# One copy and a DMA for the rows of negative maxima, a lead of seven heads, and the bins' fills on SyncE

## The reference

```python
x = x + L0_xattn(layernorm(x), ctx, mask_BxSxS2_bf1)      # 2 heads of 64
x = x + L0_ffn(layernorm(x))                              # token mix, sigmoid gate, relu squared
x = x + L1_xattn(layernorm(x), ctx, ctx, mask_Bx1xSxS2)   # 16 heads of 8
x = x + L1_ffn(layernorm(x))                              # 8 experts, each token goes to one
```

```python
scores = jnp.einsum('bhsd,bhtd->bhst', qh, kh) / math.sqrt(8)
scores = jnp.where(mask == 0, -1e9, scores)
attn = jax.nn.softmax(scores, axis=-1)                    # over 512 keys
out = jnp.einsum('bhst,bhtd->bhsd', attn, vh)
```

## Time and profile before

| | us |
|---|---|
| median of 3 runs | 298.65 |
| the three runs | 297.97, 298.65, 302.39 |
| span of the profiled execution (first to last instruction) | 296.5 |
| TensorE busy | 258.6 (87%) |
| VectorE busy | 187.7 (63%) |
| ScalarE busy | 144.1 (49%) |
| GpSimd busy | 92.3 (31%) |
| L700, the copy of the rows, 16 of them | 16.0 |
| L716, exp, 64 of them | 65.2 |

### The profile page before, as it was taken

How to read it: one execution, slowest core, us unless ns; L and a number is a source line. 1 busy time by engine, 2 the same in 40 slices (tenths; PEclk the granted TensorE clock), 3 DMA queues, 4 the chain that set the end, 5 groups by cost and what they waited for, 6 DMA issues and landing times.

```text
span 296.5 us, 5874 instructions
## 1 busy us (share of the span) xinstructions
PE 258.6 (87%) x2048; PEld 129.6 (44%) x2048; DVE 187.7 (63%) x659; ACT 144.1 (49%) x273; POOL 92.3 (31%) x108
## 2 busy tenths in 40 slices
PE   0799998697598999999998999999999888959991
PEld 0345666365353344444433334332444345625550
DVE  3290966849889767678778568664777146724440
ACT  1178465524045656656466356562576533414440
POOL 2643692603403400003300112000214642577533
PEclk9999999879799999999999799995999999988997
DMA  6990456241464689620004999520101893369500
GB/s 177 410 413 20 123 133 158 53 133 35 108 160 110 149 263 271 147 88 2 0 2 143 308 419 309 135 70 9 38 0 37 302 367 85 100 182 362 181 20 7
DMA packets 20812, 44.69 MB, mean 151 GB/s; under 512 B 1670, under 2 KB 15757, under 8 KB 19824
## 3 DMA queue, kind: packets, MB, share of 16 engines
q1 hardware_dynamic: 9296, 30.63, 32.5%
q10 hardware_dynamic: 9824, 10.00, 12.8%
q0 software_dynamic: 1664, 3.69, 3.5%
HBM read 30.90 MB, written 13.93 MB: 151 GB/s over the span
## 4 chain that ended last, share of the span: by engine, by line
PE 47%; DVE 8%; ACT 7%; issue 4%; DMA 3%; POOL 1%; POOLq 0%; DVEq 0%
PE banks L1310 11%; PE banks L1296 8%; PE banks L1226 7%; PE banks L1291 5%; PE banks L1376 5%; DVE scores_unused L977 4%; ACT p_region L716 4%; ACT q_region L700 3%; PE banks L1091 2%; PE banks L1403 2%; DMA binned_dram<-token_rows,mask_bias 1%; DMA q_region<-binned_dram,mask_bias 1%; PE banks L1097 1%; PE banks L1392 1%; PE banks L1383 1%
## 5 line engine op out<-in xcount | busy, mean ns | idle before, releaser
L977 DVE CUSTOM_DVE_ANT_0 scores_unused<-banks,mask_bias 128x512 bf16<-128x512 f32 x128 | 82.9, 688 | 25.9 <-PE banks L1226 25.1
L716 ACT ACTIVATE p_region<-banks 128x1024 f32<-128x1024 f32 x64 | 65.2, 1021 | 59.7 <-PE banks L1296 59.7
L487 POOL TENSOR_TENSOR ln_rstd<-ln_var_eps,minus_half 128x2 f32<-128x2 f32 x16 | 12.2, 765 | 117.0 <-DVE ln_var_eps L785 117.0
L1226 PE MATMUL banks<-k_region,q_region 80*128 80x512 bf16 x128 | 41.7, 397 | 2.0 <-DVE max L977 1.4
L1296 PE MATMUL banks<-q_region,k_region 80*128 80x256 bf16 x256 | 39.6, 278 | 0.0
L1310 PE MATMUL banks<-p_region,values 128*9 128x256 f32 x512 | 35.9, 403 | 2.3 <-DVE mask_bias L903 2.3
L1296 PEld LDWEIGHTS banks<-q_region,k_region 80*128 80x128 bf16 x256 | 20.0, 98 | 16.6 <-issue 15.0
L1291 PE MATMUL banks<-mask_bias_by_key,ident_bf 64*64 64x512 bf16 x256 | 26.7, 407 | 0.6 <-ACT q_region L700 0.6
L1376 PE MATMUL banks<-k_region,q_region 128*64 x64 | 23.0, 483 | 1.5 <-ACT q_region L747 0.8
L569 POOL DMA_INDIRECT binned_dram<-token_rows,mask_bias x8 | 8.2, 1023 | 51.3 <-issue 51.3
L1377 PE MATMUL banks<-k_region,q_region 128*64 128x352 f32 x64 | 23.0, 483 | 0.0
(11 more groups left out here) (146 smaller groups left out, 439.2 us busy)
## 6 DMA issues: line engine op xcount, KB each, us to landing
binned_dram<-ctx_region ACTq DMA_DIRECT2D x2, 4626.0 KB, 26.5
k_region<-experts_dram SPq DMA_DIRECT2D x17, 544.0 KB, 4.7
k_region<-k_parts_dram SPq DMA_DIRECT2D x4, 1152.0 KB
k_region<-experts_dram SPq DMA_DIRECT2D x1, 3808.0 KB, 19.5
q_region<-q_parts_dram SPq DMA_DIRECT2D x12, 192.0 KB
k_region<-mask1k_dram SPq DMA_DIRECT2D x1, 2048.0 KB, 12.0
k_region<-mask_dram SPq DMA_DIRECT2D x1, 2048.0 KB, 16.2
k_parts_dram<-q_region SPq DMA_DIRECT2D x4, 384.0 KB, 2.8
```

Of the source, the lines that this page charges most:

```text
L716: a.activation(pt[:, u % 2, j, :, :].rearrange("p (c t) q -> p c (t q)", c=2), ps[:, c:c + 2, :], ACT.Exp, scale=float(D1) ** -0.5).then_i ...
L977: return v.tensor_tensor_reduce(out=junk[:, q, :], in0=scores, in1=m1b[:, QT * (u // 4) + q, :], scale=1.0, scalar=-3e38, op0=ALU.add, op1 ...
L1226: return m.matmul(out, qst[0:R, (u * GH + j) * SQ + q * P:(u * GH + j) * SQ + (q + 1) * P], kst[0:R, (u * GH + j) * SK:(u * GH + j + 1) * ...
```

## The change

- `minus_max_rows(u)` copies the turned rows once, to a new SBUF tensor `nmrow` (8 x 2 x 256, two buffers). A DMA that ScalarE issues, `minus_max_to_heads(u)`, repeats them into the four query blocks. ScalarE waits for its own copy before it issues the DMA, and from unit 2 on for an earlier DMA before it writes the buffer. `scores_k(u, 0)` waits for the DMA (`rows_in_q`) in place of the copy.
- `turn_max(u + 1)`, the copy and the DMA stand at head 1 of unit u, one head earlier.
- LEAD is 7 in place of 6; 14 query-side scores stand in stage one, 4, 5 and 5 in slots 15, 16 and 17. `minus_maximum` comes at head 0 of a unit in place of head 1.
- The two fills of the bins are issued by SyncE: the first behind `keys_back(3)` and ahead of `queries_out(2)`, the second behind the first part of the experts' weights.

```diff
--- before.py
+++ after.py
@@ -96,9 +96,8 @@
 EARLY0 = beside0(EARLY_AT, {2: [("mix", 0)]})
 LATE0 = beside0(LATE_AT, {5: [("c1k", 0)], 7: [("c1", 0)], 9: [("c1k", 1)], 10: [("c1", 1)], 13: [("c1k", 2), ("c1", 2)],
                           14: [("c1k", 3), ("c1", 3)]})
-FIRST_Q = {15: (0, 4), 16: (4, 8), 17: (8, 12)}
-LEAD = 6
-BINS_FILLED_AT = {(2, 0): 0, (8, 0): 1}
+FIRST_Q = {15: (0, 4), 16: (4, 9), 17: (9, 14)}
+LEAD = 7
 BESIDE1 = {
     (0, 0): [("wo", 3)], (0, 1): [("s2", 3)], (0, 2): [("vv", 2)],
     (1, 0): [("s3", 2), ("n2", 3)], (1, 1): [("n3", 2)], (1, 2): [("l3T", 2)], (1, 3): [("l2T", 3)],
@@ -154,7 +153,7 @@
         for j in range(GH):
             if j == 0 and u >= 1:
                 jobs.append((f"W{u - 1}", "A"))
-            if j == 2 and u + 1 < UNITS:
+            if j == 1 and u + 1 < UNITS:
                 jobs.append((f"X{u + 1}", "M"))
             if j == 3 and u >= 1:
                 jobs.append((f"O{u - 1}", "M"))
@@ -247,6 +246,7 @@
         rd0 = sb("inv_sum0", [P, N0])
         mx1 = sb("max1", [P, 2, QT, GH])
         nm1 = sb("neg_max1_parts", [P, 2, QT, 2, GH], BF16)
+        nmrow = sb("neg_max1_rows", [MROWS, 2, SQ], BF16)
         rden = sb("inv_sum1", [P, 2, QT, GH])
 
         def W(name):
@@ -319,7 +319,7 @@
         vones = sem("values_ones")
         nm_hi, rd_done = sem("neg_max1_high"), sem("inv_sum1_done")
         sq_ready, sq_used = sem("score_q_ready"), sem("score_q_used")
-        negmax1 = sem("negmax1")
+        negmax1, rows_in_q = sem("negmax1"), sem("neg_max_rows_in")
         st_ready, exp1 = sem("score_k_ready"), sem("exp1")
         moe_w_in, blank_set, ids_set = sem("moe_w_in"), sem("blank_set"), sem("ids_set")
         bins_blank = [sem(f"bins_blank{ph}") for ph in range(2)]
@@ -416,6 +416,11 @@
                     sp.dma_start(qst[at:at + SPLIT * D1, b * H1 * SQ:(b + 1) * H1 * SQ],
                                  scrQ[b].rearrange("j (d h) n -> d j (h n)", h=H1)).then_inc(q_in[b], 16)
 
+            def blank_bins(ph):
+
+                sp.dma_start(bins_d[ph].rearrange("(s p) c -> p s c", p=P),
+                             blank.unsqueeze(1).broadcast_to([P, BINS_ROWS[ph] // P, ROW])).then_inc(bins_blank[ph], 16)
+
             keys_out(0)
             keys_back(0)
             keys_out(1)
@@ -433,11 +438,14 @@
             queries_out(1)
             sp.wait_ge(m1k_conv, B)
             keys_back(3)
+            sp.wait_ge(blank_set, 2)
+            blank_bins(0)
             queries_out(2)
             queries_out(3)
 
             sp.wait_ge(st_ready, 2 * GROUPS * GH)
             sp.dma_start(moe_w[:, 0:7 * EXPERT], moe_d[:, 0:7 * EXPERT]).then_inc(moe_w_in, 16)
+            blank_bins(1)
             sp.wait_ge(st_ready, 3 * GROUPS * GH)
             sp.dma_start(moe_w[:, 7 * EXPERT:], moe_d[:, 7 * EXPERT:]).then_inc(moe_w_in, 16)
 
@@ -696,8 +704,15 @@
 
                 arrived(act, f"X{u}")
                 src = half(f"X{u}")[:, 0:P].bitcast(BF16)[0:MROWS, :]
-                dst = qst[0:MROWS, u * GH * SQ:(u + 1) * GH * SQ].rearrange("p (j q) -> p j q", j=GH)
-                emptied(a.activation(dst, src.unsqueeze(1).broadcast_to([MROWS, GH, SQ]), ACT.Copy), f"X{u}")
+                if u >= 2:
+                    act.wait_ge(rows_in_q, 16 * (u - 1))
+                emptied(a.activation(nmrow[:, u % 2, :], src, ACT.Copy), f"X{u}")
+
+            def minus_max_to_heads(u):
+
+                copied(act, f"X{u}")
+                act.dma_start(qst[0:MROWS, u * GH * SQ:(u + 1) * GH * SQ].rearrange("p (j q) -> p j q", j=GH),
+                              nmrow[:, u % 2, :].unsqueeze(1).broadcast_to([MROWS, GH, SQ])).then_inc(rows_in_q, 16)
 
             def copy_out(u):
 
@@ -717,18 +732,15 @@
                              ACT.Exp, scale=float(D1) ** -0.5).then_inc(exp1, 1)
 
             minus_max_rows(0)
+            minus_max_to_heads(0)
             for u in range(UNITS):
                 for j in range(GH):
                     if j == 2 and u >= 1:
                         copy_out(u - 1)
-                    if (u, j) in BINS_FILLED_AT:
-                        ph = BINS_FILLED_AT[u, j]
-                        act.wait_ge(blank_set, 2)
-                        act.dma_start(bins_d[ph].rearrange("(s p) c -> p s c", p=P),
-                                      blank.unsqueeze(1).broadcast_to([P, BINS_ROWS[ph] // P, ROW])).then_inc(bins_blank[ph], 16)
                     exps(u, j)
-                    if j == 2 and u + 1 < UNITS:
+                    if j == 1 and u + 1 < UNITS:
                         minus_max_rows(u + 1)
+                        minus_max_to_heads(u + 1)
                     for kind, b in BESIDE1.get((u, j), []):
                         beside(kind, b)
 
@@ -1275,14 +1287,14 @@
 
                 b, n = u // 4, 4 * u + j
                 if j == 0:
-                    copied(pe, f"X{u}")
+                    pe.wait_ge(rows_in_q, 16 * (u + 1))
                 if u % 4 == 0 and j == 0:
                     pe.wait_ge(m1k_conv, b + 1)
                 if n >= 2:
                     pe.wait_ge(exp1, n - 1)
                 else:
                     for c in range(2):
-                        copied(pe, f"QS{2 * LEAD - 4 + 2 * n + c}")
+                        copied(pe, f"QS{max(k for k in range(2 * LEAD) if k % 4 == 2 * n + c)}")
                 first = 2 * (j % 2)
                 for c in range(2):
                     for half in range(2):
```

## The result

The changed kernel takes 324.9 us (median of four runs, 321.2 to 329.7) against 298.6 before: the ratio is 1.087, with a 95% interval of 1.079 to 1.094. I had forecast 302.7 us and a range of 295.5 to 308. The loss has the sign that I gave 0.31; with 26.3 us it is almost three times the 9.4 us that the upper end of my range allowed. Measured again on another chip, the ratio is 1.080 (1.072 to 1.089), 322.9 us. The rows of after come from that second measurement (span 322.2 us against 296.5), since the first profile of it fell in an execution slower than the rest (span 327.8 us, mean granted clock 0.888 against 0.918).

A forecast was written before the change was run, and what follows sets the result against it. TensorE was taken as the bound. The terms -3.7 -0.5 +4.3 +1.8 +0.4 +1.7 gave +4.0 us on a span of 296.5, so 300.5, and with 2.2 around it 302.7 us; range 295.5 to 308.

The forecast's parts named there:

- the sign that I gave 0.31: Chance that the changed kernel comes out slower by more than two per cent, above 304.6 us: 0.31.
- What bounds the kernel: Loop over heads: TensorE is the bound, so a shorter ScalarE instruction is worth only what TensorE waits for it.
- The term of turn_out, -3.7: In nine units turn_out waits until the copy frees bank M; with the earlier turn it no longer waits: -3.7 us.
- The landing, +4.3: Unit boundaries: scores_k waits for the row DMA under load, landing 4.1 us beside a fill, 4.6 beside weights: +4.3 us.
- Weights block it: Boundary 9: row DMA waits for all queued weight pieces, landing after about 9 us; 310.7 us in all, chance 0.16.
- The start, +1.8: Loop start: later turn, copy and DMA landing move the first masks from 86.51 to 88.6; +1.8 us, bounds 1.4 and 3.8.
- The one-hot, +0.4: At (8,0) and (12,0) weigh waits for VectorE's one-hot; minus_maximum now comes ahead of it: +0.4 us, bounds 0 and 0.8.
- The clock, +1.7: A 1.7 us wait at boundary 9 likely brings another short half-speed stretch of TensorE: +1.7 us, bounds -1.7 and +3.4.
- The issue on ScalarE, "about 0.4 us": Each unit: issuing the row DMA was priced by SyncE's small one, about 0.4 us; ScalarE's added work 0.9 against 1.0.
- The fills' move, nothing: The two fills leave ScalarE's queue; no compute waits on their issue, so the move itself was given no time.

The follow-up runs named there:

- e1: Kernel before with only the order changed (lead of seven, maxima turned at head 1); ScalarE still writes all four query blocks and issues the fills: 300.7 us, 1.007.
- f2: Changed kernel with the wait for the rows behind the mask matmuls, these repeated at units 0, 1, 2 and 9: 320.5 us, 1.070.
- e2: Kernel before with only the two fills moved to SyncE's queue: 299.0 us, 1.005.
- e3: Changed kernel with only the fills given back to ScalarE at heads (2, 0) and (8, 0): 343.2 us, 1.151.

## Why the prediction was wrong

The sum had +4.0 us and the spans differ by 25.7. Three terms make up the difference: the landing of the row DMA (+4.3, measured 14.0), the clock (+1.7, measured 10.8 in the loop) and turn_out (-3.7, measured about nothing once the layer work is counted). In the first two the mechanism was right and the size wrong; in the third a wait was left out.

**What bounds the kernel**: right. TensorE is the bound, and ScalarE's saving of 8 us is worth nothing.

**The term of turn_out, -3.7**: what failed is "Turn_out no longer waits", taken for the whole effect. It is true, but its bounds, 0 and -4, left out that place M is a queue of jobs: whatever comes behind the turn waits instead. In nine units that is layer work of head 1, 4.2 us with the short copy (0.46 each) and 9.9 with the long one (e1). BESIDE1 in the code and the place of these jobs stood before me. I priced the job behind the turn in the old order and not the one behind it in the new.

**The landing, +4.3**: the step with the largest error. The mechanism was right, and the stretches but for boundary 11, by which the second fill was through; the prices of 4.1 us beside a fill and 4.6 beside the weights were not. Against 0.3, 0.7, 1.7, 0.4 and 1.2 us at boundaries 1, 2, 9, 10 and 11 stand 3.9, 1.6, 6.2, 2.4 and 0, in sum 14.0 against 4.3. From issue to masks: 7.7 us beside the last of the keys' 16 KB pieces and the fill (97.36 to 105.02), 5.4 beside the first fill and 6.9 beside the second, 10.1 beside the weights. I charged a late start of two or three pieces; the traces show 4.0 to 5.4 us without a packet whatever the pieces' size, and then, beside the weights, 5 us more. That the waits weren't longer still is due to the slack: 3.7 to 4.5 us between issue and the moment when TensorE stood idle, where I had 2.9 and the layer work. The rival "Weights block it" had the 6 us of idle at boundary 9 right, at 0.16, but not its reason: the row DMA didn't wait for all the weight pieces. Even its 310.7 us is 14 short. Its argument against itself, two queues side by side, came from a row where both were deep.

**The start, +1.8**: first masks at 91.2 instead of 88.6, of which 3.4 us is a longer half-clock stretch ahead of the loop (busy, so 1.7 lost). From issue to masks it took 2.2 us there, as forecast (2.0).

**The one-hot, +0.4**: each wait grew by 0.4, the first too, so 0.8: at the upper bound.

**The clock, +1.7**: I named the right trigger and counted one fall, where the loop has four short ones and one of 17 us, behind a one-hot wait that was there before. The bound of +3.4 was taken from the longest stretch that I had seen, and nothing limited it to that: 10.8 in this execution, and more in the first profile. How this splits from the waits is open, since f2 didn't separate them.

**The issue on ScalarE, "about 0.4 us"**: 0.70, and 1.32 at the start. Six times copy_out waited for it, 4.9 us in all, and TensorE waited for copy_out in four places of the loop, 1.5 us (0.20, 0.25, 0.25 and 0.79), where it has no such wait before.

**The fills' move, nothing**: right (e2), and it was not idle: without it the kernel takes 18 to 20 us more (e3).

## What to carry to other kernels

A DMA put in place of a copy costs its latency under the heaviest traffic of its surroundings, not on quiet engines: look at which large transfers overlap each of its issues and how large their pieces are, and pace them, or don't put it on the path. Cutting their pieces took off 4.3 of 10.1 us here and left the late start of 4. When a job moves in a shared buffer's order, price the one that now stands behind it. And ask first whether anyone waits for the instruction at all: moving this one by half a head gave 3%, and shortening it to a third gave nothing.

## What the runs showed of the hardware

- A DMA issued behind a fill of 4626 KB in pieces of 1028 B on the same queue holds the issuing engine: 19.0 to 19.8 us on SyncE (after, e2), 5.8 and 16.8 us on ScalarE (e3), for instructions that otherwise take 0.3 to 0.7.
- A DMA of 16 KB in 32 pieces of 512 B holds ScalarE's queue for 0.70 us, 1.32 the first time, while SyncE issues one of 128 rows in 0.4.
- The same DMA needs 10.1 us from issue until TensorE goes on beside pieces of 30 KB, 5.8 beside pieces of 4 KB, 5.4 and 6.9 beside those of 1 KB, and is never waited for on quiet engines with 3.0 us and more to land in. Beside any of them none of its packets moves in the first 4.0 to 5.4 us, against 1.2 on quiet engines.
- Idle waits of 1.6 us were followed by anything from no fall of TensorE's clock to 17.1 us at half.
